# Moving work of the first token group: the last weight block's up low parts, two statistics, the second weight's preparation and the second group's projection input

## Time and profile before

| what | value |
|---|---|
| median of 3 runs | 847.41 us (847.1 to 848.42) |
| profiled execution | 848.19 us |
| its span | 846.4 us |
| TensorE busy | 825.9 us (98%) |
| VectorE busy | 583.9 us (69%) |
| ScalarE busy | 331.5 us (39%) |
| GpSimd busy | 149.6 us (18%) |
| chain that ended last | TensorE 88%, VectorE 4%, ScalarE 3% |

### The profile page before, as it was taken

How to read it: one execution, slowest core, us unless ns; L and a number is a source line. 1 busy time by engine, 2 the same in 40 slices (tenths; PEclk the granted TensorE clock), 3 DMA queues, 4 the chain that set the end, 5 groups by cost and what they waited for, 6 DMA issues and landing times.

```text
span 846.4 us, 11191 instructions
## 1 busy us (share of the span) xinstructions
PE 825.9 (98%) x4168; PEld 440.4 (52%) x4168; DVE 583.9 (69%) x947; ACT 331.5 (39%) x544; POOL 149.6 (18%) x242
## 2 busy tenths in 40 slices
PE   6997999999999999999999999999999999999997
PEld 4443476345853458443774347534485345844366
DVE  7888753778666966678766775777866696744535
ACT  5985636334234341333423343234333434122331
POOL 5324100233012220122201231022301222000000
PEclk9998999999999999999999999999999999999999
DMA  9821125110150002300032000510115000220004
GB/s 278 305 85 55 46 101 185 40 46 29 51 175 26 26 25 102 124 26 26 26 128 97 26 26 26 184 41 29 47 37 188 25 1 1 98 103 1 0 2 149
DMA packets 19191, 63.18 MB, mean 75 GB/s; under 512 B 2496, under 2 KB 4256, under 8 KB 18864
## 3 DMA queue, kind: packets, MB, share of 16 engines
q1 hardware_dynamic: 19120, 62.33, 21.3%
HBM read 45.54 MB, written 16.78 MB: 74 GB/s over the span
## 4 chain that ended last, share of the span: by engine, by line
PE 88%; DVE 4%; ACT 3%; issue 2%; DMA 1%; DVEq 1%; SPq 0%; POOL 0%; ACTq 0%; POOLq 0%
PE g L1290 26%; PE u L1290 24%; PE g L1508 4%; PE u L1508 4%; PE zb L1449 4%; PE u L1517 4%; PE g L1517 4%; PE g L1515 4%; PE u L1515 4%; PE g L1341 3%; PE mb L1378 1%; ACT w_sq L567 1%; DMA xf<-in_x 1%; PE g L1511 1%; PE u L1511 1%
## 5 line engine op out<-in xcount | busy, mean ns | idle before, releaser
L567 ACT ACTIVATE sil<-g,winv 128x512 f32<-128x512 f32 (+1 forms) x176 | 119.9, 683 | 273.7 <-PE g L1341 244.4
L889 DVE SCALAR_TENSOR_TENSOR h<-u,winv,sil 128x512 f32<-128x512 f32 x168 | 125.7, 749 | 117.7 <-ACT sil L567 101.2
L1290 PE MATMUL g<-xt,w_h 128*128 128x512 f16 x656 | 197.1, 382 | 0.0
L1290 PE MATMUL u<-xt,w_h 128*128 128x512 f16 x656 | 196.0, 380 | 0.0
L1290 PE MATMUL g<-xt,w_l 128*128 128x512 f16 x328 | 124.8, 381 | 0.0
L1290 PE MATMUL u<-xt,w_l 128*128 128x512 f16 x328 | 124.6, 380 | 0.0
L832 DVE CUSTOM_DVE_ANT_0 junk<-xn,abc 128x1024 bf16<-128x1024 f32 x96 | 120.3, 1253 | 6.0 <-issue 2.7
L1290 PEld LDWEIGHTS u<-xt,w_h 128*128 128x128 f16 x656 | 64.4, 98 | 78.1 <-issue 1.1
L1290 PEld LDWEIGHTS g<-xt,w_h 128*128 128x128 f16 x656 | 55.6, 98 | 84.5 <-issue 34.0
L464 POOL TENSOR_TENSOR ve<-mv,three 128x1 f32<-128x1 f32 x30 | 6.1, 203 | 472.2 <-DVE mv L814 472.2
L1040 DVE SCALAR_TENSOR_TENSOR ob<-xr,c_mean,gg 128x1024 f32<-128x1024 f32 x27 | 34.7, 1284 | 58.1 <-ACT gg L567 35.4
(11 more groups left out here) (258 smaller groups left out, 1144.6 us busy)
## 6 DMA issues: line engine op xcount, KB each, us to landing
xr<-in_x SPq DMA_DIRECT2D x32, 512.0 KB, 4.7
out_x<-ob SPq DMA_DIRECT2D x31, 512.0 KB, 2.9
xf<-in_x SPq DMA_DIRECT2D x30, 512.0 KB, 3.2
raw_w<-in_w2t SPq DMA_DIRECT2D x1, 2560.0 KB
abc<-in_a SPq DMA_DIRECT2D x1, 2048.0 KB, 8.0
raw_w<-in_w1t SPq DMA_DIRECT2D x2, 768.0 KB, 8.6
raw_w<-in_w3t SPq DMA_DIRECT2D x2, 768.0 KB, 10.0
base_b<-in_w2t SPq DMA_DIRECT2D x2, 512.0 KB, 4.8
```

The source lines that it names most:

```text
L567: return nc.scalar.activation(out, in_, f, **kw)
L889: stt(out=h[0:n, p % NH, :], in0=up, scalar=winv[0:n, 3 * block_of(p) + 1:3 * block_of(p) + 2], in1=sil[0:n, p % 2, :], op0=ALU.mult, op1= ...
L1290: o = mm(bank[:], a, x, start=opens and t == 0, stop=closes and t == len(terms) - 1)
```

## The change

Five steps of the first group are moved; no instruction is added or removed.

- `LOW_AT`: the two low pieces of the last block's up half go from pair 12 to pair 14 on VectorE.
- `STATS_AT`: the statistics of the second group's tile 2 go from pair 10 to pair 9, those of tile 3 from pair 14 to pair 15.
- `BASE_AT`: the additions with the second row go from pairs 15 and 16 to 17 and 18.
- `W2_AT` and `W2L_AT`: ScalarE's high parts 3, 4 and 5 of the second weight go from pairs 18, 19, 20 to 19, 20, 21, and VectorE's low parts 0 and 1 from pairs 16 and 18 to 19 and 20.
- TensorE: `second_z0` goes behind all of `down_high(1)`.

```diff
-        STATS_AT = [(3, 7, 10, 14)] + [(1, 7, 13, 19)] * (NG - 1)
+        STATS_AT = [(3, 7, 9, 15)] + [(1, 7, 13, 19)] * (NG - 1)
...
-        W2L_AT = {16: 0, 18: 1}
+        W2L_AT = {19: 0, 20: 1}
...
-        BASE_AT = {10: (0, 0), 12: (1, 0), 15: (0, 1), 16: (1, 1)}
+        BASE_AT = {10: (0, 0), 12: (1, 0), 17: (0, 1), 18: (1, 1)}
...
-                  11: ((3, 0, 0), (3, 0, 1)), 12: ((3, 1, 0), (3, 1, 1))}
+                  11: ((3, 0, 0), (3, 0, 1)), 14: ((3, 1, 0), (3, 1, 1))}
...
-        W2_AT = {13: 0, 15: 1, 16: 2, 18: 3, 19: 4, 20: 5}
+        W2_AT = {13: 0, 15: 1, 16: 2, 19: 3, 20: 4, 21: 5}
...
                     down_high(0, range(3, HN))
-                    down_high(1, range(0, 3))
+                    down_high(1, range(0, HN))
                     second_z0()
-                    down_high(1, range(3, HN))
                     down_low(0)
```

## The result

The changed kernel takes 841.94 us (median of 6 runs, 841.59 to 842.71); the kernel before, with six runs by now, 847.85 us (846.99 to 849.69). The ratio is 0.9931, 95% interval 0.9921 to 0.9941: 5.9 us faster. The forecast was 841.0, in a range of 839.2 to 844.7. The profiled execution took 841.59 us, its span is 839.8 us, 6.6 us less than before; the forecast for it was 6.4.

A forecast was written before the change was run, and what follows sets the result against it. TensorE, busy 825.9 of 846.4 us, was taken as the bound, so only its waits and slow clock have a price. 2.7 (minimum) + 3.1 (clock) + 0.6 (second z) = 6.4 us off 847.41 gave 841.0 us, range 839.2 to 844.7.

The forecast's parts named there:

- The minimum in the new order: Before line 1407's transposes: the minimum comes earlier, TensorE goes on at 73.45; 2.7 of the 4.66 us go, 2.0 stay.
- Rival 1: At the minimum: no collisions of VectorE with GpSimd, TensorE goes on at 72.2; gain 7.6 us, 839.8; chance 20%.
- rival 3: GpSimd's next sum precedes the last base addition: wait left 3.2 us; 842.2 with clock held, 845.3 down; chance 14%.
- The clock: Behind the wait at line 1407: the clock stays up after the shorter wait; gain 3.1 us, other bound 0.
- rival 2: Behind the wait at line 1407: the clock falls all the same after 2.0 us; 844.1 us; chance 13%.
- The up low pieces at pair 14: Before pair 16's up chain: two pieces of 1.0 us each, now behind the minimum, are hidden; cost 0.
- Rival 4: At pair 16: the low pieces move the wait there, TensorE stands 4.7 us, the clock falls; 848.8 us; chance 3%.
- The later places of the rest: Pairs 15 to 21: tile 3's statistics, second-row base additions and w2 parts, moved later, cost 0, at most 0.5 us.
- The second z: Before line 1423, at the scale copy: TensorE's 0.63 us wait goes; gain 0.6 us, bounds 0 to 0.8.

The follow-up runs named there:

- the filled wait: Kernel before plus twenty extra 128x512 products on TensorE, results overwritten, ahead of the transposes that wait for the minimum: 845.43 us, ratio 0.9977.
- the one edit alone: Kernel before with only the last block's two up low pieces moved from pair 12 to pair 14: 842.46 us, ratio 0.9931.
- the best version: Changed kernel with tile 2's statistics back at pair 10 and the second base addition moved to pair 14: 839.86 us, ratio 0.9909.

## Why the prediction was right

- **The minimum in the new order.** Forecast: TensorE goes on at 73.45, a wait of 2.0; measured 73.17 and 1.76. The rebuilt line holds in what it rests on: GpSimd's sum runs behind the base addition, the low part is 1.76 long (forecast near 1.8), the next base addition gets ahead of GpSimd's next sum. In one place the order was another: GpSimd's difference ran before product 11's addition and not behind it, so the addition was held, and the low pieces of the gate half began at 67.24 instead of 67.5. The order at the second base addition was less certain than it came out: the forecast had it at 70.75 and the sum at about 70.8; the sum came at 71.29. Rival 1 (no collisions, 0.7) and rival 3 (3.2) fall by the wait; putting tile 2's statistics back shows that they are a cover and that their move costs half a us.
- **The clock.** It held behind 1.76 us, as forecast and against rival 2, and the filled wait shows the cause of the fall. That it would hold behind the forecast's 2.0 us is another matter: the forecast took it from the 1.5 us of the earlier trace rows, and in a later profile it fell behind 1.95 us (line 1508). So this part was right with some luck, since the wait came out at 1.76, below the longest that was seen to hold (1.87). **The size is the term that was off**: 3.1 us from the one profiled execution of before. The two profiles differ by 2.9; the 0.2 too much is in the transposes, where the forecast set a duration of 1.08 us against a step of 0.44 in the chain, while the duration at the full clock is 0.63. The filled wait gives 2.1 in the median. With 2.1 in place of 3.1 the forecast's sum is 5.4, with 2.9 it is 6.2; 5.9 was measured.
- **The baseline.** Of the 0.9 us by which 841.94 lies above the forecast 841.0, 0.4 is the kernel before: its median was 847.41 with three runs and 847.85 with six.
- **The up low pieces at pair 14.** No wait at line 1308: the two ended at 77.4 and 78.4, 0.4 later than forecast, and TensorE came to the first of them at 79.25. Rival 4 did not occur.
- **The later places of the rest.** Cost 0, as forecast, and gain 0 (with these steps back, 841.66 us). Product 21 ended 0.2 us before the batch at line 1449 asked (forecast margin 0.3). ScalarE's and VectorE's tail was later by the 0.8 forecast: with the second z in its old place the wait is 1.44 and no longer 0.63.
- **The second z.** Forecast +0.6, measured 0.63 of wait gone. The forecast set it against the old wait; within the changed order the move is worth 1.4, since it also covers the 0.8 that the other moves add.

What the forecast did not say is that the parts besides the low pieces cancel. The statistics of tile 2 cost 0.56 us and the second z gives 0.63; the one edit alone does as well.

## What to carry to other kernels

When a bank is overwritten behind a reader on another engine, list what stands in front of that reader and put behind it whatever is due later. A wait may cost its length and 2 to 3 us more in clock, and the second part goes as a whole once the wait is short enough. Then look at the waits that are just under that length as well: one of 1.4 to 1.9 us in the middle of this kernel grew to 1.95 in one execution of the best version, and what that cost was as much as the version had gained over the changed kernel. Before filling an idle half us of VectorE, see which of its instructions run beside GpSimd's: the statistics did, and moving them away cost more than they filled.

## What the runs showed of the hardware

- In dense work the clock stayed up behind waits of 0.36, 1.18, 1.20, 1.44 and 1.76 to 1.77 us in the first group and of 1.43 to 1.87 us at line 1508. It was at half behind 1.95 us at line 1508 (one execution) and behind 3.77, 4.66 and 5.22 us. Between 1.95 and 3.77 there is no row.
- The price of a fall differed with the time until the clock came back: 2.2 us behind the 5.22 us wait, 2.7 behind 3.77, 2.9 behind 4.66 (each from the end of the wait to pair 16's first product, less 3.93), and 1.5 behind 1.95. The longest of these waits did not cost the most clock.
- A VectorE instruction with two inputs in SBUF and one of GpSimd that reads SBUF exclude each other for whole instructions, and the one that waits comes next: a base addition of 1.28 us lasted 1.74 or 2.28, a small low piece of 0.28 lasted 1.28, a sum of 1.27 lasted 2.10. This exclusion is what the Trainium skill says ("SBUF — State Buffer", section "Who interferes with whom").
- One input is no guarantee of running free. The statistics (0.69 us) and the minimum, which reads PSUM (0.68), kept their length beside GpSimd, but the comparison of line 873, with one small input in SBUF, lasted 0.60 us in the profile of the change, until GpSimd's sum of 72.97 had ended, and 0.17 in that of before.
